# A stored turned context for the third and fourth layers, sixteen query transfers, and a reordered third layer

## What is computed

```python
def _L1_xcond_ref(x, u, ...):            # second layer, u = ctx_1024; L3 likewise with context = ctx_1024
    x = x + mha(xn, xn, xn, sa_qw, ...)
    x = x + mha(x, u, u, ca_qw, ca_qb, ca_kw, ca_kb, ca_vw, ca_vb, ca_ow, ca_ob)
...
def _L0_xcond_ref(x, c, context, ...):
    q_c = _ln(x) @ W_qc + b_qc
    kv_c = _ln(context) @ W_kvc + b_kvc
...
def _L2_xcond_ref(mix_hidden_states, global_anchor, prototype_bank, ...):   # prototype_bank = ctx_1024
    q = nx @ Wq
    k = prototype_bank @ Wk
    v = prototype_bank @ Wv
    scores = jnp.einsum('bth,bph->btp', q, k) * H ** (-0.5)
    weights = jax.nn.softmax(scores, axis=-1)
    evidence = jnp.einsum('btp,bph->bth', weights, v)
```

## Time and profile before

| | us |
|---|---|
| median of 3 runs (6243.02 to 6251.53) | 6248.7 |
| the profiled execution | 6255.5 |
| its span in the profile | 6253.2 |
| TensorE busy, share of the span | 83% |
| VectorE busy, share of the span | 61% |
| ScalarE, GpSimd busy | 48%, 23% |
| mean granted clock of TensorE, full speed is 1 | 0.881 |

### The profile page before, as it was taken

One profiled execution on the slowest core, in us unless ns is written; L12 is line 12 of the kernel. 1 busy time (PEld: TensorE's weight loads), 2 busy tenths in 40 slices (PEclk: granted clock), 3 DMA queues, 4 the chain that ended last, 5 costly groups with the idle time before them and its releaser, 6 DMA issues. The chain is left out here.

```text
span 6253.2 us, 151177 instructions
## 1 busy us (share of the span) xinstructions
PE 5213.4 (83%) x64126; PEld 3352.7 (54%) x64126; DVE 3844.1 (61%) x7732; ACT 3016.4 (48%) x4479; POOL 1458.3 (23%) x758
## 2 busy tenths in 40 slices
PE   4838999999985849999999877779675799999998
PEld 3614555555653615666666545555353466666664
DVE  4537888888744527777777623334353577777773
ACT  2324666666652315666666532212322366666665
POOL 2024444444302022333222000000201223332220
PEclk7667999999996669999999977779766799999999
DMA  3325545555403345555555211110141555555540
GB/s 76 63 64 156 158 157 164 164 164 158 147 17 65 64 110 162 165 164 165 164 167 164 73 33 48 48 38 1 44 77 28 171 165 165 165 164 164 164 152 15
DMA packets 544827, 717.59 MB, mean 115 GB/s; under 512 B 183450, under 2 KB 457402, under 8 KB 531770
## 3 DMA queue, kind: packets, MB, share of 16 engines
q1 hardware_dynamic: 535322, 696.87, 38.4%
q10 hardware_dynamic: 8832, 11.07, 0.8%
HBM read 441.82 MB, written 264.09 MB: 113 GB/s over the span
## 5 line engine op out<-in xcount | busy, mean ns | idle before, releaser
L1247 DVE TENSOR_REDUCE maxima<-ps 100x1 f32<-100x482 f32 (+1 forms) x4608 | 2720.2, 650 | 896.3 <-PE ps L1092 886.6
L1202 ACT ACTIVATE probs<-ps 128x800 f32<-128x800 f32 (+1 forms) x2304 | 1800.5, 835 | 655.6 <-PE ps L1113 653.9
L1092 PE MATMUL ps<-kst,qst 48*100 48x482 bf16 (+1 forms) x4608 | 1117.7, 411 | 107.1 <-DMA qst<-cross_q_parts 51.3
L1299 POOL TENSOR_TENSOR kparts<-kf,zero 128x1444 bf16<-128x1444 f32 x192 | 498.3, 2595 | 2280.3 <-ACT kf L1174 2250.9
L1130 PE MATMUL ps<-probs,vals 128*9 128x100 f32 x36864 | 1012.4, 250 | 7.9 <-ACT probs L1202 0.8
L1113 PE MATMUL ps<-qst,kst 128*128 128x200 bf16 (+1 forms) x9216 | 999.6, 250 | 11.7 <-DMA qst<-nparts 5.5
L1113 PEld LDWEIGHTS ps<-qst,kst 128*128 128x128 bf16 (+1 forms) x9216 | 759.0, 98 | 251.2 <-issue 124.7
L1130 PEld LDWEIGHTS ps<-probs,vals 128*9 128x9 f32 x36864 | 734.3, 90 | 259.6 <-issue 219.2
L1092 PEld LDWEIGHTS ps<-kst,qst 48*100 48x100 bf16 x4608 | 341.7, 119 | 630.2 <-DVE maxima L1247 329.9
L1180 ACT ACTIVATE vals<-ps 128x512 f32<-128x512 f32 (+1 forms) x288 | 161.9, 562 | 467.1 <-PE ps L1075 467.1
L1064 PE MATMUL ps<-ident,ctok 128*128 128x128 f32 (+1 forms) x1152 | 195.6, 292 | 210.2 <-DMA ctok<-in_ctx_dram 108.7
(11 more groups left out here) (256 smaller groups left out, 4951.3 us busy)
## 6 DMA issues: line engine op xcount, KB each, us to landing
kst<-ctx_k_stack SPq DMA_DIRECT2D x96, 2888.0 KB
ctx_k_stack<-kparts SPq DMA_DIRECT2D x192, 541.5 KB
ctx_k_stack<-kparts SPq DMA_DIRECT2D x192, 361.0 KB
ctok<-in_ctx_dram SPq DMA_DIRECT2D x96, 704.0 KB
ctx_k_stack<-kparts SPq DMA_DIRECT2D x192, 180.5 KB
c<-in_ctx_dram SPq DMA_DIRECT2D x32, 704.0 KB
o_sums<-osb SPq DMA_DIRECT2D x96, 200.0 KB
qst<-cross_q_parts SPq DMA_DIRECT2D x1152, 12.5 KB
```

The lines of the kernel that those rows point to most:

```text
L1092: nc.tensor.matmul(ps[0:N, at:at + w], g.qst[s][row0:row0 + CROWS, j, N * e:N * e + N], g.kst[s][row0:row0 + CROWS, j, a:a + w], start=Tru ...
L1202: nc.scalar.activation(probs[kt % 2][hf][0:kts[kt], :].rearrange("p (k n) -> p k n", k=2), src, ACT.Exp).then_inc(exp_done, 1)
L1247: nc.vector.reduce_max(maxima[:, col:col + 1], ps[0:N, at:at + widths[c]], AX.X).then_inc(m_read, 1)
L1299: return nc.gpsimd.tensor_tensor(out, src, g.zero[0:src.shape[0], 0:1].to_broadcast(list(src.shape)), ALU.add)
```

## The change

The second layer's cross-attention (`context == "raw"`) writes each batch's turned context to a new array in memory, `ctx_turned`, by one DMA of 128 x 1444 fp32. The third layer's attention loads it beside the context as it was and leaves out its transposes and ACT copies. The fourth layer's cross-attention (`context == "kept"`) loads only the turned context, has no T tiles, and places the six remaining tiles behind six different steps. The queries' array is laid out by chunks, so that 16 DMAs write it where 64 did; the 12 loads for each batch read 100-token pieces out of rows of 400. In the third layer TensorE now has the scores of batch b+2 between the second and the third group of the weights' turning, and DVE takes the maximum of b+2 before it normalizes b+1. GpSimd's key split is in three column ranges in layers 2 and 4.

```diff
 def sp_queries_out(g, sp, parts, low, stored):
-    per = CH // N
     for c in range(NCH):
         sp.wait_ge(low, c + 1)
         for e in range(2):
-            for j in range(per):
-                b = c * per + j
-                sp.dma_start(g.qx[b, e].rearrange("t r n -> r t n"),
-                             parts[HALF * e:HALF * e + HALF, :, N * b:N * b + N]).then_inc(stored, 16)
+            sp.dma_start(g.qx[c, e].rearrange("t r n -> r t n"),
+                         parts[HALF * e:HALF * e + HALF, :, CH * c:CH * c + CH]).then_inc(stored, 16)
...
-def cross_attention_phase(g, wk, kb, wv, normed):
+def cross_attention_phase(g, wk, kb, wv, context):
...
-    S1 = 9
+    normed, kept = context == "normed", context == "kept"
+    S1 = 6 if kept else 9
+    CUTS = [(0, S)] if normed else [(0, BANK), (BANK, 2 * BANK), (2 * BANK, S)]
...
+    if kept:
+        PREPS = {0: ("V0",), 1: ("V1",), 3: ("V2",), 4: ("K0",), 6: ("K1",), 7: ("K2",)}
+        PREP_INDEX = {"K0": 0, "K1": 1, "K2": 2, "V0": 3, "V1": 4, "V2": 5}
...
+        if kept:
+            turned = [sb(f"ctxT{s}", [P, S]) for s in range(LAG)]
+        else:
+            ctok = [sb(f"ctok{s}", [P, KT, P]) for s in range(LAG)]
+            turned = [sb("ctxT", [P, S])] * LAG
...
+                if i == 0 and not normed:
+                    wait(act, ctx_kept, 16 * b)
...
+            for i, (a, z) in enumerate(CUTS):
+                wait(pool, p_read, S1 * b + PREP_INDEX["K0"] + (i + 1 if len(CUTS) == 3 else 3))
+                done = 3 * (len(CUTS) * b + i)
+                pool_copy(parts[:, 0, a:z], kf[:, a:z]).then_inc(split, 1)
...
         def sp_load_ctx(k):
+            if kept:
+                wait(sp, p_full, S1 * (b - LAG + 1))
+                sp.dma_start(turned[s][:, :], g.ctxT[b]).then_inc(ctx_loaded[s], 16)
+                return
...
+        def sp_keep_ctx(k):
+            b, s, sp = k.b, k.s, g.sp
+            wait(sp, p_read, S1 * b + PREP_INDEX["T2"] + 1)
+            sp.dma_start(g.ctxT[b], turned[s][:, :]).then_inc(ctx_kept, 16)
...
         def sp_load(sp, k):
+            wait(sp, s_full, b - LAG + 1)
+            sp.dma_start(ctxT[s][:, :], g.ctxT[b]).then_inc(turned_loaded[s], 16)
             wait(sp, e_full, b - LAG + 1)
...
+                for b in range(B):
+                    k, k2 = known(b), known(b + 2) if b + 2 < B else None
+                    for t in range(2):
+                        pe_turn_weights(pe, k, t)
+                    if k2 is not None:
+                        pe_scores(pe, k2)
+                    pe_turn_weights(pe, k, 2)
+                    pe_evidence(pe, k)
...
                     dve_evidence(dve, k)
+                    if k2 is not None:
+                        dve_scores(dve, k2)
                     if k1 is not None:
                         dve_normalize_weights(dve, k1)
                     dve_out(dve, k)
-                    if k2 is not None:
-                        dve_scores(dve, k2)
...
-    g.qx = nc.dram_tensor("cross_q_parts", (B, 2, PARTS, HALF, N), BF16).ap()
+    g.qx = nc.dram_tensor("cross_q_parts", (NCH, 2, PARTS, HALF, CH), BF16).ap()
+    g.ctxT = nc.dram_tensor("ctx_turned", (B, P, S), F32).ap()
```

More of the change, by code:

```diff
@@ L991, in cross_attention_phase @@
         nparts = sb("nparts", [HEADS, 3, N], BF16)
-        ctok = [sb(f"ctok{s}", [P, KT, P]) for s in range(LAG)]
-        ctxT = sb("ctxT", [P, S])
+        if kept:
+            turned = [sb(f"ctxT{s}", [P, S]) for s in range(LAG)]
+        else:
+            ctok = [sb(f"ctok{s}", [P, KT, P]) for s in range(LAG)]
+            turned = [sb("ctxT", [P, S])] * LAG
         kf = sb("kf", [P, S])
@@ L1065, in pe_prep @@
             elif name[0] == "K":
-                wait(g.pe, p_read, S1 * b + PREP_INDEX["T0"] + i + 1)
+                if kept:
+                    wait(g.pe, ctx_loaded[s], 16 * (r + 1))
+                else:
+                    wait(g.pe, p_read, S1 * b + PREP_INDEX["T0"] + i + 1)
                 a = BANK * i
                 w = min(BANK, S - a)
-                ins = nc.tensor.matmul(ps[:, at:at + w], wk, ctxT[:, a:a + w], start=True, stop=True)
+                ins = nc.tensor.matmul(ps[:, at:at + w], wk, turned[s][:, a:a + w], start=True, stop=True)
             else:
-                if i == 0:
+                if i == 0 and not kept:
                     wait(g.pe, p_read, S1 * b + PREP_INDEX["T2"] + 1)
@@ L1167, in act_prep @@
                 w = min(BANK, S - a)
-                nc.scalar.activation(ctxT[:, a:a + w], ps[:, at:at + w], ACT.Copy).then_inc(p_read, 1)
+                if i == 0 and not normed:
+                    wait(act, ctx_kept, 16 * b)
+                nc.scalar.activation(turned[s][:, a:a + w], ps[:, at:at + w], ACT.Copy).then_inc(p_read, 1)
             elif name[0] == "K":
                 if i == 0:
-                    wait(act, parts_ready, b)
+                    wait(act, parts_ready, len(CUTS) * b)
                 a = BANK * i
@@ L1371, in sp_keys_out @@
             sp = g.sp
-            wait(sp, parts_ready, b + 1)
+            wait(sp, parts_ready, len(CUTS) * (b + 1))
             for first, n in K_RUNS:
@@ L1396, in sp_slot @@
                 sp_out(slot.k(-1))
+            if context == "raw" and slot.k(3) is not None:
+                sp_keep_ctx(slot.k(3))
             if slot.k(1) is not None:
@@ L1500, in _ @@
                 sp_out(known(B - 1).k(0))
+                if context == "raw":
+                    sp.wait_ge(ctx_kept, 16 * B)
                 for s in range(LAG):
@@ L1567, in l2_attention_phase @@
         ctx_loaded, u_ready = [sem(f"ctx_loaded{s}") for s in range(LAG)], sem("u_ready")
-        t_full, t_read = sem("turned_full"), sem("turned_read")
+        turned_loaded = [sem(f"turned_loaded{s}") for s in range(LAG)]
         s_full, mx_done, nmx_done, exp_done, inv_done, p_norm = (sem("scores_full"), sem("max_done"), sem("negmax_done"),
@@ L1581, in pe_scores @@
             b, s, r = k.b, k.s, k.r
[L1582 to L1589 removed]
+            wait(pe, turned_loaded[s], 16 * (r + 1))
             wait(pe, u_ready, b + 1)
[L1591 removed]
             wait(pe, exp_done, b)
@@ L1617, in act_scores @@
             b, s, r = k.b, k.s, k.r
-            for t in range(3):
-                wait(act, t_full, 3 * b + t + 1)
-                a = BANK * t
-                w = min(BANK, S - a)
-                if t == 0:
-                    wait(act, s_full, b)
-                nc.scalar.activation(ctxT[s][:, a:a + w], ps[:, T_BANK + BANK * (t % 2):T_BANK + BANK * (t % 2) + w],
-                                     ACT.Copy).then_inc(t_read, 1)
             wait(act, nmx_done, b + 1)
```

76 lines of the change are left out of this document (30 added, 46 removed).

## The result

| | before | after |
|---|---|---|
| median, us (4 runs each) | 6249.8 (6243.0 to 6251.5) | 5854.4 (5850.7 to 5862.1) |
| ratio, 95% interval | | 0.9371 (0.9355 to 0.9387) |
| profiled execution | 6255.5 | 5862.1 |
| its span | 6253.2 | 5859.9 |
| mean granted clock of TensorE | 0.881 | 0.897 |

The change takes 395 us from the median; forecast were 398, and 5851 us. The span fell by 393.3 us. Where they went can be read from three marks that a layer leaves in SP's timeline: the first query store, the first negative maximum of the slots and the last one (32 of them). The table is of the two profiled executions.

The account below looks back on a forecast made before the run. Bounds: SP's store issue in query stages, TensorE's chain and lowered clock in the third layer, TensorE with DVE in fourth-layer slots. 94 + 231 + 73 = 398 us off the profiled 6255.5 gives 5857.5, median 5851 us; range 5825 to 5945.

Parts of the forecast that it names:

- Queries, 94 us: Query stages of three layers: 48 of 64 stores go, saving 31.4 us a layer, 94 us in all.
- 0.655 us over 0.85 and 1.44: Candidate prices of one larger query store; they save 94, 85 or 57 us in all, and 0.655 was taken.
- Rival 2: Query stores are bound by data, so the 94 us don't come: 5945 us, chance 0.05.
- Third layer, 231 us: Third layer's attention: a batch falls from 15.28 to 7.75 us at full clock over 31 batches, saving 231 us.
- the 7.7 to 7.9 us that were named as a sign: Third layer: expected spacing of exponentials, with the clock 1.00 in most stretches.
- rival 1: TensorE's clock keeps falling in the third layer: 9.8 us a batch, 170 us saved, 5912 us; chance 0.17.
- Fourth layer, 73 us: Fourth layer: 2.4 us less in each of 29 slots, 70 us, plus the first batch's transposes: 73 us.
- The 2.92 us for the first batch's transposes: Fourth layer's start: the first batch no longer waits 2.92 us for its transposes.
- Rival 4: Fourth layer gains nothing, as six lone visits cost as much as the five shared ones: 5924 us, chance 0.05.
- Second layer, 0: Second layer: the added context store and GpSimd's smaller key splits cost 0, at worst 10 us for the store.
- rival 3: SP's query loads cost 1.44 us each and bound the slots: 6324 us, slower from about 1.37 a load; chance 0.02.
- The lower end of the range, 5825: Favourable bounds for the whole kernel: a slightly cheaper store, 7.65 us a batch, 2.7 us a slot.

Follow-up runs that it names:

- run 1: Kernel before the change with only the 16 query stores, the new query layout and its loads: 6167.9 us, ratio 0.9864.
- run 4: Changed kernel, third layer turning its context itself on TensorE in the new order, with four context buffers: 5936.8 us, ratio 0.949.
- run 2: Changed kernel, third layer loading the turned context but keeping the old order on TensorE and VectorE: 6016.7 us, ratio 0.962.
- run 8: Changed kernel with preparation tiles in other steps of the first, second and fourth layers, K1 and K2 together in step 7: 5819.2 us, ratio 0.9304.
- Run 5: Changed kernel with the fourth layer's six tiles in the old places, in four visits: 5858.3 us.
- run 7: Changed kernel, second layer storing its turned context twice, into two arrays: 5848.1 us.
- run 6: Changed kernel with GpSimd splitting the keys in one piece in every layer: 5876.0 us.
- runs 2 to 5 and 11: Includes two not listed singly: changed kernel, third layer turning its context itself in new order, three buffers (6148.5 us); changed kernel repeated (5859.3 us).
- run 9: Kernel of run 8 with half of each layer's 16 query stores issued from ACT's queue: 5811.1 us, ratio 0.9294.

## Why the prediction was right, step by step

*Queries, 94 us.* 31.1 us for each layer from the start of the stage to the cross-attention's first load (44.62 to 13.48 us in the first), 93.4 together. In run 1, where they stand alone, the three starts gain 90.8 us and the medians 85; the second layer's start, below, is a part of that difference. The choice of 0.655 us over 0.85 and 1.44 was right: the stores were 0.66. Rival 2 is refuted. So is the estimate from the Trainium skill's figures (DMA: Bandwidth & Descriptors, Bandwidth), 1.4 us a store: its table is of single loads issued by GpSimd, while what counted here was how often SP could issue a store.

*Third layer, 231 us.* It was 240. The mechanism held with the term a little too small: I allowed 7.75 us, and the batch is 7.42. The exponentials stand closer than the 7.7 to 7.9 us that were named as a sign. The 0.1 us for DVE's normalization was not needed, and my sum of TensorE's pieces, taken from starts in the earlier trace rows, counted the two groups, the scores and the third group 0.85 + 2.48 + 1.29, where they are 0.74 + 2.43 + 1.23. That the load of 740 KB for each batch costs nothing was right: TensorE's waits from 3670 to 3900 us (total, times, longest) are the one for the copy and two at the start, and none is for `cT`, at a DMA share of 0.58:

```profile
PE ps L1638 <- DVE pT L1674: 21.7, 30, 0.7
PE ps L1618 <- ACT pq L1646: 6.6, 2, 3.6
```

*The clock, rival 1.* TensorE still pauses 0.72 us in each batch, and the clock is 0.98. In run 4 it pauses 0.25, 0.66 and 0.72 us, and the clock is 0.99. In run 2 it pauses 1.75 us, works 0.56 and pauses 0.72, and the clock is 0.71. The experiments show that the order closed the long wait and that the clock came back with it. The Trainium skill (TensorE: Matmul & The Clock Gate, A second HAM failure mode) lets short idles between groups of matmuls make the clock swing; here idles of 0.72 us did not.

*Fourth layer, 73 us.* It was 65.7, all in the slots. The 2.92 us for the first batch's transposes did not reach the first negative maximum. The maxima of the first batch do begin 3.1 us earlier than in run 1 (56.44 us after the first query store instead of 59.55), but up to the turning of the row maxima they then take 40.85 us instead of 37.74. From 60 to 80 us after the first load TensorE's clock is 0.50, and in run 1 it is 0.82 and then 1.00; the tiles in between are others too, so which of the two took the 3.1 us back is open. The slot lost 2.22 us, not 2.4, as the sum of two errors. Six lone visits cost 7.35 us above plain steps where I had 7.0 (V2 alone costs 1.44, and no run here looked for the reason), and nothing was over for the copy that V0 and V1 had paid for, for which I had allowed 0.28. On the other side the turning step fell from 3.69 to 3.25 us, which I had not seen. In run 8 it falls in the first two layers too, when K1 and K2 are put in step 7, right ahead of it. Rival 4 is refuted. Run 5 puts 1.96 of the 2.22 us to the tiles' removal and 0.26 to their spreading.

*Second layer, 0.* The steady slots are at 38.41 us, with a store more in them, and run 7 shows room for a second one. But its start gained 25.3 us and not 31. My first thought after the result was that the twelve smaller splits or the stores cost 6 us. Three runs refute it: run 1 has neither and run 6 has one piece, and they are at 103.5 and 103.6 us, run 7 with two stores at 102.9. With the second layer's code of the changed kernel five other profiles (runs 2 to 5 and 11) lie between 102.7 and 105.7, so none comes near the 98.8 that the kernel before would have with a stage 31.1 us shorter. What differs in the profiles is the clock in the first slots, as the section on the hardware shows. The cuts cost nothing, as forecast, but they are a condition for the fourth layer's places (run 6), and the prediction gave them no part in it.

*SP, rival 3.* Its price was 1.37 us a load, and a load costs 0.70 as before. (The working took a slot as 38.4 us in all three layers; the first layer's is 40.35, which makes the loss smaller: by the same working about 344 us instead of 400, and the price about 1.42.) The mechanism is real, however: in run 6 it was GpSimd's splitting that made SP late, SP set the slot, and the kernel lost some 20 us.

*The sum.* 94 + 231 + 73 = 398, measured 89.7 in the three starts, 240.3 in the third layer, 65.7 in the fourth layer's slots, less 2.4 of small differences elsewhere: 393.3 in the profiles. The terms were off by 4 us too much, 9 too little and 7 too much, so that the total came out within 3 us of the median is in part luck. The lower end of the range, 5825, was also further down than the favourable terms named for it: 7.65 us a batch and 2.7 us a slot make 5840.

## What to carry to other kernels

A wait on the bounding engine costs more than its length where TensorE's clock falls behind it: in a batch of 12.12 us with a wait of 1.75 us in it, the lower clock cost 3 us more in the mean, and the same work in another order without the wait (10.14 us) had a clock of 0.99. When work is moved forward in an order, look up when the buffer that it reads comes free; three buffers were enough for the old place and one too few for the new, and that turned a gain of 159 us into a loss of 49. A stage that only issues transfers was priced here by their number, until the engine that feeds them and the landing of the last one set its end (run 9).

## What the runs showed of the hardware

I had not expected the starts of the cross-attentions to vary as they do. The first layer's code is the same in the changed kernel and in the runs 1 to 7 and 11, and from first query store to first negative maximum its profiles have 110.9 (run 7), 111.2 (run 5), and from 114.7 to 116.5 us in the others. What differs is the granted clock while the first tiles are prepared. In the second layer, 111 to 131 us after the first query store of the kernel before, and 80 to 100 us after it in the changed kernel, whose query stage is 31 us shorter (columns as in the earlier trace rows):

```profile
2331.70:2341.70 10.00, 8.84 (x34) 3.72 (x32) 7.34 (x13) 3.49 (x7) 0.00 (x0) 1.00 0.28 77
2341.70:2351.70 10.00, 7.34 (x18) 2.12 (x17) 9.22 (x20) 0.79 (x2) 8.88 (x4) 0.71 0.00 1
```

```profile
2266.66:2276.66 10.00, 9.34 (x31) 4.53 (x30) 6.15 (x11) 2.36 (x5) 0.00 (x0) 0.67 0.57 179
2276.66:2286.66 10.00, 9.63 (x18) 2.89 (x17) 6.12 (x11) 1.98 (x3) 8.38 (x8) 0.50 0.00 1
```

Before, the clock was 1.00 and 0.71 there, afterwards 0.67 and 0.50. The stretches hold about the same work. In the first layer, where the code is identical, it goes the same way: 90 to 100 and 100 to 110 us after the first query store the clock is 1.00 and 0.76 in run 7 (110.9 us) and 0.67 and 0.59 in the changed kernel (116.19). But no run changed the clock alone, so that it is the cause of the 5 us is argued and not shown; nor is it known how often the kernel before has the shorter start, since there is only one profile of it. Whoever compares two profiles of this kernel should not read a difference of up to 5 us in a start as the work of a change.
